# The tile of points and terms of an eigenvalue search, moved from PSUM to SBUF, in a graph-network kernel

## The reference, cut to what matters

```python
def _L0_gnn_ref(x, adj, Wg0, bg0, Wg1, bg1, Wih, Whh, bih, bhh):
    h = jax.nn.relu(jnp.einsum('ts,bsh->bth', adj, x @ Wg0 + bg0))
    h = jax.nn.relu(jnp.einsum('ts,bsh->bth', adj, h @ Wg1 + bg1))
    for p in range(1, MAX_SKIP + 1):
        ...
        last = _lstm_last(Wih[p - 1], Whh[p - 1], bih[p - 1], bhh[p - 1], wins)
        ...

def _L2_gnn_ref(features, A, W1, b1, W2, b2):
    ...
    L_norm = d_inv_sqrt[:, None] * L * d_inv_sqrt[None, :]
    _, U = jnp.linalg.eigh(L_norm)
    agg = jnp.einsum('mn,bnd->bmd', U.T, features)
    ...
```

## Time and profile before

| | |
|---|---|
| median of 3 runs | 4685.79 us (4685.65 to 4686.28) |
| the profiled execution, its own time | 4684.37 us |
| its span | 4682.6 us |
| DVE busy over the span | 3723.7 us (80%) |
| PE / ACT / POOL busy over the span | 3243.1 / 1335.7 / 951.9 us |
| the search, 2410 to 3465 us: DVE / ACT / POOL busy | 992.42 / 483.22 / 264.57 us of 1055 us |

### The profile page before, as it was taken

The page is one execution under the profiler, slowest core; times in us unless marked ns, Lnnn a source line. Parts: engine busy times, 40 slices in busy tenths (PEclk is TensorE's granted clock), DMA queues, the critical chain, the costliest instruction groups (busy, mean ns, idle before and its releaser), DMA issues. The chain is left out here.

```text
span 4682.6 us, 77138 instructions
## 1 busy us (share of the span) xinstructions
PE 3243.1 (69%) x21375; PEld 2287.7 (49%) x21375; DVE 3723.7 (80%) x20826; ACT 1335.7 (29%) x4374; POOL 951.9 (20%) x3459
## 2 busy tenths in 40 slices
PE   4677676666666666666658667677956999757764
PEld 4666665555555555566643233332223666523522
DVE  6888898888877777777789999999997995343476
ACT  2333323333333333333324255444431111011000
POOL 2232232223233333222210024322310000000000
PEclk9955555555555555555559889898977999889856
DMA  2000000000000000000000000000000000000001
GB/s 74 2 2 2 2 2 2 1 2 2 2 1 1 1 1 1 1 1 1 1 1 1 1 1 1 1 1 1 1 1 1 1 1 1 0 0 0 0 0 36
DMA packets 14192, 17.63 MB, mean 4 GB/s; under 512 B 408, under 2 KB 10047, under 8 KB 13759
## 3 DMA queue, kind: packets, MB, share of 16 engines
q1 hardware_dynamic: 13758, 12.67, 1.0%
HBM read 8.47 MB, written 4.19 MB: 3 GB/s over the span
## 5 line engine op out<-in xcount | busy, mean ns | idle before, releaser
L611 PE MATMUL totals<-pp_sum,ones 128*128 128x2 f32 x768 | 225.4, 363 | 473.0 <-DVE pp_sum L418 473.0
L1128 DVE SCALAR_TENSOR_TENSOR lanes<-lanes,rows,poly 128x60 f32<-128x60 f32 x2048 | 482.0, 281 | 8.2 <-DVE poly L1147 0.5
L1136 DVE SCALAR_TENSOR_TENSOR poly<-poly,off,lanes 128x60 f32<-128x60 f32 x2048 | 477.2, 270 | 0.0
L573 PEld LDWEIGHTS product<-x_parts,A_parts 128*128 128x128 bf16 x11136 | 435.4, 111 | 56.9 <-DVE A_parts L356 42.6
L573 PE MATMUL product<-x_parts,A_parts 128*128 128x3 bf16 x11136 | 420.8, 168 | 42.9 <-DVE A_parts L356 41.6
L611 PEld LDWEIGHTS totals<-pp_sum,ones 128*128 128x128 f32 x768 | 192.3, 311 | 505.7 <-DVE pp_sum L418 505.7
L532 POOL TENSOR_SCALAR x_scaled<-vwv,sc 128x4 f32<-128x4 f32 (+3 forms) x510 | 175.7, 344 | 1063.2 <-DVE prod_x L375 508.8
L899 PE MATMUL gate_ps<-h_sb,u 128*128 128x512 f32 (+1 forms) x504 | 324.3, 755 | 18.3 <-ACT gate L1016 18.3
L662 ACT ACTIVATE vwv<-v,sc 128x8 f32<-128x8 f32 (+3 forms) x510 | 152.3, 299 | 582.3 <-DVE sc L397 557.1
L562 PE MATMUL coef<-x_on_pairs_sum,ones 128*128 128x4 f32 (+30 forms) x988 | 305.9, 403 | 1.1 <-DVE x_on_pairs_sum L471 0.2
L566 PE MATMUL row_e<-vwv,first 128*128 128x2 f32 (+28 forms) x924 | 282.5, 396 | 0.0
(11 more groups left out here) (498 smaller groups left out, 8210.4 us busy)
## 6 DMA issues: line engine op xcount, KB each, us to landing
out_dram<-x_sb SPq DMA_DIRECT2D x4, 1024.0 KB, 7.3
adj_sb<-adj_dram SPq DMA_DIRECT2D x1, 1024.0 KB, 5.3
alpha<-L_gnn_alpha_train_dram SPq DMA_DIRECT2D x1, 256.0 KB
w<-L_gnn_Wg_dram SPq DMA_DIRECT2D x2, 64.0 KB
w<-L_gnn_W_dram SPq DMA_DIRECT2D x2, 64.0 KB
edge_row<-L_gnn_src_dram SPq DMA_DIRECT2D x1, 128.0 KB
edge_row<-L_gnn_dst_dram SPq DMA_DIRECT2D x1, 128.0 KB
x_sb<-x_dram SPq DMA_DIRECT2D x4, 0.5 KB, 10.7
```

The lines of the kernel that those rows point to most:

```text
L573: last = pe.matmul(product[:, r, 0:PARTS], parts[:, i, c, r * P:(r + 1) * P], x_parts[:, c, :], start=(c == c0 and i == 0), stop=(c == C - ...
L611: pe.matmul(totals[:, 0:2], k.ones[:], pp_sum[:], start=True, stop=True).then_inc(dot_ready, 1)
L1128: pair(dve.scalar_tensor_tensor(out=term[:, way, :], in0=flat, scalar=rows[:, way, row:row + 1], in1=poly[:, b, way, s + 1, :], op0=ALU.su ...
L1136: pair(dve.scalar_tensor_tensor(out=poly[:, b, way, s + 2, :], in0=poly[:, b, way, s, :], scalar=off2[:, way, row:row + 1], in1=term[:, wa ...
```

## The change

`lanes` becomes an SBUF tile of 180 columns, and `all_passed` a PSUM tile of its own. `flat`, `cut` and `term` are views of `lanes` as before and move with it. No engine has an instruction more or less, and their order is the same on each: lines 1109, 1128, 1136 and 1188 have operands elsewhere, and lines 926 and 1182 use the tile `all_passed`.

```diff
-        lanes = ps("lanes", [P, N])
+        lanes = sb("lanes", [P, 3 * L])
...
         cut = lanes[:, 0:L].rearrange("p (g j) -> p g j", j=CUTS)
         term = lanes[:, L:3 * L].rearrange("p (w l) -> p w l", w=2)
-        all_passed = lanes[:, 3 * L:3 * L + C]
+        all_passed = ps("all_passed", [P, C])
...
-            pair.now(dve.scalar_tensor_tensor(out=k.lam[:], in0=all_passed, scalar=width[:], in1=k.lam[:],
+            pair.now(dve.scalar_tensor_tensor(out=k.lam[:], in0=all_passed[:], scalar=width[:], in1=k.lam[:],
                                               op0=ALU.mult, op1=ALU.add))
```

## The result

The changed kernel takes **4884.99 us** in the median of 3 runs (4882.76 to 4885.06), against 4685.79: ratio 1.0423, 95% interval 1.04 to 1.0447. It is slower by 199 us. The profiled execution took 4882.76 us, its span is 4881.0.

What follows compares the result with a forecast made beforehand. The prediction took DVE to set the time of the search, and summed 4684.4 us (the profiled execution) + 16 (the beat) + 185 (the stops, net) to 4885 us, with a range from 4830 to 4960.

Steps and rivals of the forecast that it cites:

- The bound: In the search, DVE sets the time; nobody makes it wait, and ACT and PE run behind with room.
- The beat: Start to start of lines 1128 and 1136 in the search: 191.4 ns against 187.5, +16 us over 4096 instructions.
- The stops: Lines 1128 and 1136, with two SBUF tensor inputs, wait until POOL's instruction is done: +213 us, net +185.
- 0.14 + 0.08 us: Taken off each POOL instruction's length: 0.14 from two observed waits, 0.08 for DVE's next instruction starting after POOL begins.
- the collisions: Two DVE instructions, lines 1142 and 1140, seen waiting for POOL in the earlier trace, losing 0.88 and 0.89 us.
- The short lines: Lines 1133, 1140, 1142 and 1147 in the search: 23 us of excess already paid, which should remain or shrink.
- The first: Rival: SBUF is the faster place for lines 1128 and 1136, 133 ns start to start, 4646 us; chance 0.06.
- The second: Rival: POOL does not stop lines 1128 and 1136, leaving 4700 us, or 4684 at equal pace; chance 0.05.
- The third: Rival: back-to-back DVE instructions keep POOL out until a block's end, delaying PE, ACT and DVE: 4990 us; chance 0.08.

Runs made afterwards that it cites:

- the quiet pair: The kernel before and the changed kernel, each with POOL's tensor_tensor instructions in the search replaced by memsets of the same output: 4664.47 and 4686.26 us.
- the last kernel above: The kernel before with line 1142 removed, its work folded into lines 1133 and 1140, and line 1140's output in PSUM: 4661.39 us, ratio 0.9949.

## Why the prediction was right, point by point

- **The bound.** DVE set the time of the search before and after; its waits at the ends of blocks did not change.
- **The beat.** Predicted 191.4 ns from the same form at 4 and at 512 wide, measured 191.9. As a time: +16 forecast, 17.0 from 4096 x (191.92 - 187.77) ns, and 17.1 in the blocks of the quiet pair, where it stands alone. The Trainium skill's table ("VectorE: DVE Perf Modes", section on the TRN2 errata), by which, as estimated, SBUF operands would have gained 265 us, does not hold for these instructions: the trace has SBUF 4 ns slower.
- **The stops.** Predicted +213 us in all, 28 paid before, net +185. Measured 208.7 in all, 29.4 before, **net +179**. The steps inside were off in both directions. What is taken off a POOL instruction's length was forecast as 0.14 + 0.08 us. For the 225 stopped instructions the loss is what is left of POOL's instruction less 0.19 us (0.189 to 0.201), and they start 0.095 us behind it in the mean, which is half of the beat: 0.29, so 16 us too much in the sum. POOL's own work was taken as 264.57 us and became 275.00, so 10 too little. The 0.14 came from a tensor_tensor and a tensor_scalar with constants; the form with a pointer scalar was not in the collisions that were read. In the last kernel above line 1140 is a scalar_tensor_tensor without a pointer, and its six stops cost what was left less 0.135 us, which points at the pointer.
- **The rest.** The short lines lost their excess altogether (the prediction allowed "remain or shrink"), because their meetings became meetings of the long lines: 231 stops in the search for its 231 large POOL instructions. DVE's three waits for the last count, at the ends of sweeps (line 1167), fell from 5.5 to 2.0 us, for which the forecast had no term. With it the search is accounted for: 17.0 + 179.3 - 3.5 = 192.8 of the 193.0 us that it became longer.
- **The rivals.** The first fell with the beat. The second fell with 225 long instructions in lines that had none. The third fell with POOL's gaps and DVE's waits: between lines 1075 and 1076 there is no gap, POOL's group means grew by 0.04 us on average, and even twice the POOL work left DVE's waits as they were.

POOL's groups after, which show the last point (their counts are those of the kernel before):

```profile
L1059 POOL TENSOR_TENSOR h_sb<-gate,squashed 128x512 f32<-128x512 f32 (+1 forms) x36 | 44.7, 1241 | 122.3 <-ACT squashed L1006 122.3
...
L1075 POOL TENSOR_TENSOR neg<-gate 128x512 f32<-128x512 f32 (+1 forms) x36 | 43.0, 1194 | 311.8 <-ACT gate L1016 311.8
...
L1076 POOL TENSOR_TENSOR cell<-gate,cell 128x512 f32<-128x512 f32 (+1 forms) x36 | 40.0, 1111 | 0.0
```

That 4885 was met within 1 us is luck beside this. Inside the stops, errors of 16 and 10 us cancelled in part. For the search the forecast of 16 + 185 = 201 us is 8 too much, and the 5.4 us outside the search that were taken as scatter made up for most of it. What the rows carried is the size of two terms to some 10 us.

## What to carry to other kernels

Where DVE is the bound and POOL works beside it, count the tensor inputs that each DVE instruction takes from SBUF: in this kernel a second one made it wait for whatever tensor_tensor POOL had under way on SBUF, and back-to-back instructions then paid for three quarters of POOL's time (208.7 of 275.0 us). A PSUM tile for one of the two operands avoids it and cost nothing in pace here. Look for such stops in the largest duration of a line and in its mean against its median, since they stand inside the instruction and not in an idle time.

## What was not expected

- Four times the stops from twice the POOL work (29.4 to about 126 us in the whole search, with PSUM): meetings with a few short instructions depend on their phase, and come in rows where POOL's chain has no gap.
- Line 1128 has a shorter median duration with all operands in SBUF (273 against 281 ns, line 1136 has 272 against 269), and yet the beat of the two is longer (191.9 against 187.8 ns). A duration is not the time that an overlapped instruction takes.
- An instruction with two SBUF inputs goes past a POOL memset without a stop, while one of the one-input kind (1133, 1161, 1162) is stopped by it too, for up to 0.39 us.
